# A state-space mixer with a LoRA feed-forward: TensorE's waits one product earlier, and work of the second batch moved between engines

## The reference

```python
proj = hidden_states @ in_proj_w.T
gate, hBC, dt = jnp.split(proj, [INTER, INTER + CONV_DIM], axis=-1)
hBC = silu(causal_conv4(hBC) + conv_b); hs, Bx, Cx = split(hBC)
dt = softplus(dt + dt_bias); A_dt = A * dt; A_cs = cumsum(A_dt) in each chunk
M = (Cc Bc^T) * exp(segsum(A_dt))          # mask of decays in a chunk
Y_diag = M X                               # X = hs * dt
states = (Bc * exp(A_cs[-1] - A_cs))^T X   # one state a chunk, passed on
Y_off = (Cc prev_states) * exp(A_cs)
xg = (Y_diag + Y_off + D * hs) * silu(gate)
xr = xg * rsqrt(mean over the 1024 channels of a group + EPS)
return (xr * norm_weight) @ out_proj_w.T
```

## Time and profile before

| | |
|---|---|
| median of 3 runs | 1581.26 us (1580.66 to 1581.79) |
| profiled execution | 1580.66 us, its span 1578.9 us |
| first batch, a step between group ends | 10.78 us |
| second batch, a step between group ends | 10.78 us |

### The profile page before, as it was taken

How to read it: one execution, slowest core, us unless ns; L and a number is a source line. 1 busy time by engine, 2 the same in 40 slices (tenths; PEclk the granted TensorE clock), 3 DMA queues, 4 the chain that set the end, 5 groups by cost and what they waited for, 6 DMA issues and landing times.

```text
span 1578.9 us, 29209 instructions
## 1 busy us (share of the span) xinstructions
PE 1559.5 (99%) x9172; PEld 1271.9 (81%) x9172; DVE 1414.5 (90%) x2343; ACT 1367.7 (87%) x2620; POOL 1291.1 (82%) x1614
## 2 busy tenths in 40 slices
PE   8999999999999999999999999999999999999998
PEld 7877888888888888887778788888888888888886
DVE  6988999999999999999979898898898888888887
ACT  4678899999999999989846899999999999999996
POOL 5549998999999998989874488778787878787786
PEclk9999999999999999999999999999999999999999
DMA  5257767676776676766614666766667667667673
GB/s 178 94 171 223 197 214 221 196 226 195 220 225 198 213 224 199 220 202 208 198 42 142 201 198 222 218 201 225 212 200 230 200 210 222 199 221 215 202 225 92
DMA packets 231754, 311.83 MB, mean 197 GB/s; under 512 B 144176, under 2 KB 160560, under 8 KB 231344
## 3 DMA queue, kind: packets, MB, share of 16 engines
q1 hardware_dynamic: 231600, 309.97, 63.9%
HBM read 240.69 MB, written 36.70 MB: 176 GB/s over the span
## 4 chain that ended last, share of the span: by engine, by line
PE 87%; DVE 5%; POOL 4%; issue 2%; ACT 1%; DMA 1%; SPq 0%; DVEq 0%; ACTq 0%; POOLq 0%
PE bg L804 21%; PE bo L975 20%; PE bt L804 12%; PE bh L804 11%; PE by L1031 7%; PE bg L1053 7%; PE bt L1018 3%; PE bh L1018 2%; PE bo L783 1%; POOL wl L631 1%; DVE cv L1085 1%; PE bo L862 1%; POOL xl L734 1%; DMA turned<-tg 1%; POOL wol L750 1%
## 5 line engine op out<-in xcount | busy, mean ns | idle before, releaser
L407 ACT ACTIVATE mt<-cs_row,cs_tok 128x128 f32<-128x128 f32 x1024 | 324.5, 390 | 0.0
L631 POOL TENSOR_TENSOR wl<-raw,wh 128x256 fp32r<-128x256 f32 x328 | 250.2, 792 | 59.1 <-ACT wh L379 59.1
L725 POOL COPY xt<-turned 128x512 uint16<-128x512 uint16 x248 | 202.3, 862 | 42.3 <-DMA turned<-tg 42.3
L716 POOL TENSOR_TENSOR mt<-mt,gt 128x256 f32<-128x256 f32 x128 | 118.0, 943 | 141.7 <-ACT mt L588 141.2
L741 POOL TENSOR_TENSOR sqa<-sqa,sq 128x256 f32<-128x256 f32 x222 | 223.7, 1027 | 1.0 <-ACT sq L561 1.0
L750 POOL TENSOR_TENSOR wol<-raw_o,woh 128x256 fp32r<-128x256 f32 x256 | 190.4, 764 | 10.5 <-ACT woh L528 10.5
L734 POOL TENSOR_TENSOR xl<-xg,xh 128x256 fp32r<-128x256 f32 x254 | 189.7, 768 | 6.0 <-ACT xh L541 6.0
L1085 DVE SCALAR_TENSOR_TENSOR cv<-bt,par_sb,cv 128x511 f32<-128x511 f32 (+2 forms) x192 | 143.7, 748 | 49.3 <-ACT cv L383 44.8
L1085 DVE SCALAR_TENSOR_TENSOR cv<-bh,par_sb,cv 128x511 f32<-128x511 f32 (+2 forms) x192 | 143.7, 748 | 35.4 <-ACT cv L383 30.9
L379 ACT ACTIVATE wh<-raw 128x1024 fp32r<-128x1024 f32 (+1 forms) x146 | 152.3, 1043 | 0.7 <-DMA raw<-in_w_dtag 0.7
L975 PE MATMUL bo<-woh,xl 128*128 128x512 f32 x508 | 149.1, 415 | 0.4 <-POOL xl L734 0.4
(11 more groups left out here) (215 smaller groups left out, 3814.7 us busy)
## 6 DMA issues: line engine op xcount, KB each, us to landing
raw<-in_w_step SPq DMA_DIRECT2D x128, 512.0 KB, 4.6
cs_row<-cs_rows SPq DMA_DIRECT2D x128, 512.0 KB, 7.0
low_parts<-wl SPq DMA_DIRECT2D x64, 512.0 KB, 5.8
raw_o<-in_w_out SPq DMA_DIRECT2D x128, 256.0 KB, 5.7
wl<-low_parts SPq DMA_DIRECT2D x64, 512.0 KB, 4.7
ec_row<-ec_rows SPq DMA_DIRECT2D x256, 96.0 KB, 5.7
raw<-in_w_bc SPq DMA_DIRECT2D x16, 512.0 KB, 3.6
acc<-in_x SPq DMA_DIRECT2D x8, 256.0 KB, 5.4
```

The lines of the kernel that those rows point to most:

```text
L407: e = act.activation(mt[:, m % 2, h, chunk(j)], cs_row[:, m % 2, h, chunk(j)], ACT.Relu, bias=cs_tok[:, j, 2 * m + h:2 * m + h + 1], scale ...
L631: e = pool.tensor_tensor(wl[:, n % 2, cols], raw[:, n % 2, cols], wh[:, n % 2, cols].bitcast(F32), ALU.subtract)
L725: e = pool.tensor_copy(to[:, half], turned[:, NJ * half:NJ * (half + 1), :])
```

## The change

1. TensorE, in the iterations with `early_state`: each wait stands one product earlier. The states' wait (v_xd) stands before the last wol product, p_xl's before the last of the states, the chunk products' (v_x, v_m or p_m, v_xg) before the last product with xl, those of the products with S (and of the sum of squares) before the last chunk product, and the next step's weights before the last product with S.
2. Second batch: GpSimd masks both heads, the first ahead of the tokens' copy, the second behind xl; VectorE masks none (but for the last step).
3. Second batch: VectorE drains two blocks of a group, ScalarE and GpSimd two.
4. First batch: `keep_high` stores wh in DRAM (512 KB a step) at the end of SP's iteration, and ScalarE's next split into the same buffer awaits it. Second batch: `load_parts` loads high and low part of the step's weights; raw isn't loaded and ScalarE makes no wh there.
5. `add_bias` moves from iterations 2 to 5 to the last four B and C units of the prologue.
6. VectorE's statistics and norm of the next batch move from behind the gate and convolution products to a place ahead of the taps.

```diff
+            def keep_high(m):
+                sp.wait_ge(a_wh, did(step(0, m)))
+                sp.dma_start(high_parts[m], wh[:, step(0, m) % 2, :].bitcast(F32)).then_inc(st_high[m % 2], 16)
+
+            def load_parts(m):
...
+                sp.wait_ge(st_high[m % 2], landed(m))
+                sp.dma_start(wh[:, step(1, m) % 2, :].bitcast(F32), high_parts[m]).then_inc(ld_high[m % 2], 16)
                 sp.wait_ge(st_low[m % 2], landed(m))
                 sp.dma_start(wl[:, step(1, m) % 2, :].bitcast(F32), low_parts[m]).then_inc(ld_low[m % 2], 16)
...
+        def dve_blocks(g):
+
+            return DVE_BLOCKS if g < GROUPS else 2
...
+                    if g >= GROUPS - NJ:
+                        add_bias(b, g - (GROUPS - NJ))
...
+                        if m < STEPS:
+                            mask_decays(0)
+                        else:
+                            mask_decays(1).then_inc(p_m, 1)
...
+                    if masks and m < STEPS:
+                        mask_decays(1).then_inc(p_m, 1)
...
                                 for j in range(NJ):
+                                    if then and k == ks[-1] and j == NJ - 1:
+                                        then()
...
                         if has(m - 2):
-                            output(range(2) if early_state else range(3))
+                            if early_state:
+                                output(range(2), await_states)
+                            else:
+                                output()
...
                         for c in range(NS):
+                            if early_state and c == NS - 1:
+                                pe.wait_ge(p_xl, did(n - 2))
                             mm = pe.matmul(other[:, chunk(c)], btok[:, g, c, :], xd[:, c, :], start=True, stop=True)
                         mm.then_inc(t_st, 1)
+                        yb = bank_y(b, m - 1)
                         if early_state:
-                            output((2,))
...
+                            output((2,), await_chunks, awaited=True)
+                        else:
+                            await_chunks()
                         for j in range(NJ):
                             for h in range(2):
+                                if early_state and j == NJ - 1 and h == 1:
+                                    if ends:
+                                        await_squares()
+                                    await_off()
...
+                            if c == 1:
+                                pe.wait_ge(v_s, did(n - 1, 4, 4))
+                            if c == NS - 1 and early_state and has(m + 1):
+                                await_weights(b, step(b, m + 1))
```

More of the change, by code:

```diff
@@ L189, in did, with by_dve, by_act @@
             return n * per + (CR + (per if k is None else k))
+        def dve_blocks(g):
+            return DVE_BLOCKS if g < GROUPS else 2
+        def by_dve(g, k=None):
+            return CR + sum(dve_blocks(i) for i in range(g)) + (dve_blocks(g) if k is None else k)
+        def by_act(g, k=None):
+            return CR + sum(NJ - dve_blocks(i) for i in range(g)) + (NJ - dve_blocks(g) if k is None else k) \
+                if g >= 0 else CR
         def landed(n):
@@ L367, in _ @@
                                 .then_inc(ld_ec[m % 2], 16)
+                    if b == 0 and has(m + 1):
+                        keep_high(m + 1)
             store(NB - 1)
@@ L377, in split_hi @@
             def split_hi(n):
+                b, m = step_of(n - 2)
+                if b == 0 and m >= 0:
+                    act.wait_ge(st_high[m % 2], landed(m))
                 act.wait_ge(ld_raw[n % 2], landed(n))
@@ L477, in _ @@
                     first_tap(b, g, 1, bank_c[g % 2])
-                    split_hi(bc(b, g + 2))
+                    if b == 0 or g + 2 < GROUPS:
+                        split_hi(bc(b, g + 2))
                     if g == 0:
@@ L590, in _ @@
                             take_b(b, GROUPS - 1)
-                    if has(m) and not early_split and (has(m + 2) or b + 1 < NB):
+                    if has(m) and not early_split and b + 1 < NB:
                         act.wait_ge(t_g, did(n))
@@ L736, in _ @@
                         e.then_inc(p_xl, 1)
+                    if masks and m < STEPS:
+                        mask_decays(1).then_inc(p_m, 1)
+                    if has(m - 2) and (b + 1 < NB or has(m - 1)):
                         if (m - 2) % PER_GROUP:
@@ L791, in tokens, with await_weights, project @@
                 return lambda k: t[:, b, k, :] if j is None else t[:, b, k, chunk(j)]
-            def project(dst, b, n, kind):
-                pe.wait_ge(a_wh, did(n))
+            def await_weights(b, n):
+                _, m = step_of(n)
+                if b == 1 and m >= 0:
+                    pe.wait_ge(ld_high[m % 2], landed(m))
+                else:
+                    pe.wait_ge(a_wh, did(n))
+            def project(dst, b, n, kind, awaited=False):
+                _, m = step_of(n)
+                kept = b == 1 and m >= 0
+                if not awaited:
+                    await_weights(b, n)
                 for i, (w, t) in enumerate(((wh, xTh), (wh, xTl), (wl, xTh))):
                     if i == 2:
-                        _, m = step_of(n)
-                        if b == 1 and m >= 0:
+                        if kept:
                             pe.wait_ge(ld_low[m % 2], landed(m))
@@ L934, in sum_squares, with await_states, await_chunks, await_squares @@
                         return mm
-                    def output(ks=range(3)):
+                    def await_states():
+                        pe.wait_ge(v_xd, did(n - 1))
+                        if not by_dma(b, m - 1):
+                            pe.wait_ge(v_x, did(n - 1))
+                        if m > 2 and (m - 2) % PER_GROUP == 0:
+                            pe.wait_ge(v_ms, did((n - 2) // PER_GROUP - 1))
+                        if m == 1:
+                            pe.wait_ge(a_bt, did(b * GROUPS + (GROUPS - 1)))
+                    def await_chunks():
+                        pe.wait_ge(v_x, did(n - 1))
+                        if b + 1 < NB:
+                            pe.wait_ge(v_m, did(n - 1))
+                        else:
+                            pe.wait_ge(p_m, m)
+                            if m == STEPS:
+                                pe.wait_ge(v_m, did(STEPS))
+                        if bank_y(b, m - 1) is by:
+                            pe.wait_ge(v_xg, did(n - 2))
+                    def await_squares():
+                        pe.wait_ge(v_h2, did(un))
+                        pe.wait_ge(p_sqa, squares(b, m - 2))
+                    def await_off():
+                        pe.wait_ge(v_sg, did(min(n, b * STEPS + STEPS - 1)))
+                        pe.wait_ge(v_off, did(n - 2))
+                        pe.wait_ge(a_s1, did(n - 1))
+                        pe.wait_ge(v_s, did(n - 1, 4, 2))
+                    def output(ks=range(3), then=None, awaited=False):
                         first, very_last = (m - 2) % PER_GROUP == 0, n - 2 == NB * STEPS - 1
@@ L982, in _ @@
                             pe.wait_ge(v_h2, did(un - 4 + m))
-                        project(mine, b, step(b, m), 0).then_inc(t_hs, 1)
+                        project(mine, b, step(b, m), 0, awaited=m > 2).then_inc(t_hs, 1)
                         if m == 0:
@@ L1111, in add_group @@
                 else:
-                    dve.wait_ge(p_acc, did(g - 1, ACT_BLOCKS))
-                for j in range(1, NJ) if very_last else range(DVE_BLOCKS):
+                    dve.wait_ge(p_acc, by_act(g - 1))
+                for j in range(1, NJ) if very_last else range(dve_blocks(g)):
                     if very_last:
@@ L1329, in _ @@
                         add_group(b, ended)
-                    if has(m - 1) and not ahead:
-                        mask_decays(2 if b + 1 < NB else 1)
+                    if has(m - 1) and b + 1 < NB:
+                        mask_decays()
                     if m == STEPS and b + 1 < NB:
@@ L1334, in _ @@
                         token_lo(b + 1, 3)
+                    if b + 1 < NB and STEPS - 12 <= m < STEPS - 6:
+                        h, part_of = divmod(m - (STEPS - 12), 3)
+                        if part_of < 2:
+                            stats_of(b + 1, 2 * h + part_of)
+                        else:
+                            variance(b + 1, h)
+                    if b + 1 < NB and STEPS - NJ <= m < STEPS:
+                        norm(b + 1, m - (STEPS - NJ))
                     if has(m):
```

112 lines of the change are left out of this document (45 added, 67 removed).

## The result

| kernel | median | ratio to before | profiled execution |
|---|---|---|---|
| before | 1581.21 us (5 runs) | | 1580.66, span 1578.9 |
| changed | 1606.33 us (1604.44 to 1609.15, 5 runs) | 1.0162 (95%: 1.0147 to 1.0176) | 1604.44, span 1602.5 |

The account below looks back on a forecast made before the run. TensorE's stream plus its stalls was taken as the bound; +1.7 + 4.2 - 2.7 - 2.4 - 1.1 = -0.3 us on the profiled 1580.66 gave 1580.4, by medians 1581.0 us, range 1564 to 1589.

Parts of the forecast that it names:

- The gaps are not waits: TensorE's idle 0.37 and 0.17 us around 64-column loads come from tiling changes; sooner waits gain 0 there.
- Part 1: TensorE's waits one product sooner, ordinary steps: 0 in the first batch, +1.7 us in the second for late xd.
- Rival C: Earlier xd wait at the last wol product costs a load's delay every step: +9.8 us, 1591; chance .18.
- Part 2: Group ends of the first batch: earlier waits for xd and S prolong the stalls, +4.2 us.
- Part 3: add_bias in the prologue relieves over-full GpSimd in steps 2 to 5, shortening waits for xd: -2.7 us.
- Part 4: VectorE's next-batch statistics ahead of the taps no longer delay S: -2.4 us.
- Part 5: Second batch, less work on ScalarE and VectorE: VectorE's relief returns S waits at group ends, -1.1 us.
- Part 6: High part stored in the first batch and reloaded in the second: both fit the DMA time, 0 us.
- Rival D: First batch: storing the kept high part delays the transposes, 62 x 0.1 to 0.3 us, 1587 to 1600; chance .08.

Follow-up runs that it names:

- safe_hoists: Changed kernel with the waits for xd and S (v_xd, v_s) at their old places, all others still early; 1581.8 us, ratio 1.0003.
- off_back: Changed kernel with the waits for S, sg, off, a_s1 and the squares at their old places, xd's still early; 1591.7 us, ratio 1.0066.
- hoist_only: Kernel before with TensorE's earlier waits alone and nothing else of the change; 1605.0 us, ratio 1.0147.
- all_back: Changed kernel with all of TensorE's waits at their old places, the rest as changed; 1581.0 us, ratio 1.0004.
- no_high: stats_back without the kept high part and its reload: raw is loaded and split in the second batch again; 1579.1 us, ratio 0.9986.
- bias_only: Kernel before with only add_bias moved to the prologue; 1579.3 us, ratio 0.9992.
- stats_back: all_back with VectorE's statistics and norm behind the convolution's product again; 1578.8 us, ratio 0.9984.
- yield_xd: Changed kernel, but GpSimd starts its second mask and its squares only when xd is done; 1598.7 us, ratio 1.0110.

## Why the prediction was wrong

It forecast no change and measured +25 us. Step by step, by its own parts:

- *The gaps are not waits*: right. 46.5 and 22.4 us after, 44.4 and 21.6 in safe_hoists. The rule of the Trainium skill (TensorEngine Tiling (Array Packing), Key Properties) that a change of tiling mode drains TensorE fits all of these runs. The early waits gained nothing at the four places that safe_hoists tests (the last of the states, the last product with xl, the last chunk product without v_s, the last product with S).
- *Part 1, ordinary steps, is the step that failed.* It took 0 in the first batch for xd, "a slip once a group, not once a step", because VectorE "has 0.54 to spare before its taps". This row reads [0.54 <-ACT cv L383], and that cv is made from TensorE's own projection of the same step. Idle time that ends with the bottleneck's own product is no slack against the bottleneck: if TensorE slips, the taps slip, and xd is as late in the next step as in this one. So the delay comes back step by step and not once a group. Measured with all waits early: 0.21 a step in the first batch, 0.31 in the second. Rival C had the place and the mechanism of xd, at 0.11 a step (13.6 us) and a chance of .18; off_back, where xd is awaited early and S isn't, has just that 0.11 in most steps of the first batch and puts the wait for xd at 10.7 us. What C lacked is the wait for S.
- *The wait for S was costed only at the ends of groups*; for an ordinary step part 1 put it at nothing without a reason. It is the larger one: 26 us alone. Most of what it needed was there: the first user of S's pieces stands two recorded products behind 1214.41, and the last chunk product, the new place, ahead of it; S's own row (1213.61) isn't among the rows of the prediction. The sentence "each wait stands one product earlier" was taken over for v_s without counting that it had stood at the second product behind the change of tile, 0.53 away. Nor did the prediction name the way over ScalarE, which is what makes S late in hoist_only's second batch.
- *Part 2, group ends*, +4.2: they aren't to be told apart from the loss in every step; eight steps grew by 1.6 and 1.9 us, of which the ordinary steps make the most.
- *Part 3, bias*, -2.7: the mechanism was right, the size 1.5.
- *Part 4, statistics*, -2.4: +2.2 measured. The statistics' half was right (-1.8). The norms wait for GpSimd's rstd, and I had not asked what would be queued behind that wait.
- *Part 5*, -1.1 at the second batch's group ends from VectorE's relief: the step behind each of them went from 10.98 to 10.78 (all_back), 1.4 us in seven. But VectorE's relief alone, in no_high, changed that step and the next from 10.99 and 10.78 to 10.81 and 10.88 and the batch by 0.4 (678.51 in bias_only to 678.13); the rest came with ScalarE's relief. That the size came near is partly luck, as the relief that counted was to the larger part ScalarE's. VectorE's mask, costed at 1.0, took 0.68 to 1.26 before. That the second mask would stand beside xd and not only beside the squares wasn't seen; with the waits at their old places it costs nothing (10.78), with them early it makes 10.95 into 11.09.
- *Part 6, the store*: right within what can be told (stats_back 1578.8, no_high 1579.1), though its two halves are +1.5 and -1.3 and not 0 and 0. Rival D falls: the transposes land as before (1.38 for 1.40).

## What to carry to other kernels

A wait in front of a product costs nothing as long as what it waits for comes in time, and gives nothing by standing earlier unless something behind it is held up; so count, for each semaphore, the time between its signal and its new place in the load queue, across every product and change of tile that it is moved over. Where the awaited chain begins with the bottleneck's own output of the same step, it is a loop: add it up once round, compare it with the bottleneck's own step, and take the whole excess for every step. Do it for each engine on which such a way leads back; when one loop is shortened, the next longest is the limit. And an operation that is moved ahead of others takes its waits with it: the question is what stands behind it in that queue.

## What the runs showed of the hardware

- The gap before the first load with another tile width is the same wherever the waits stand: 0.37 us from 128 to 64 columns behind a 512-column product, 0.17 back behind chunk products of 128. A late semaphore ahead of it can hide in it in part: in yield_xd the wait for the masks held the last load of xl by 0.21, the gap behind it shrank to 0.24, and the step grew by 0.04 (10.82).
- VectorE and GpSimd beside each other: xd takes 0.55 alone, 1.13 if a GpSimd piece of 0.74 starts 0.03 ahead of it, 1.01 if it starts 0.14 ahead and 0.81 if 0.35 ahead, so the less of the piece is left, the less xd pays. xt takes 1.04 with a piece that started 0.56 ahead and was 1.05 long, 1.26 with one of 0.74 that started 0.03 ahead; the norm took 0.53 before and 1.00 where it stands now. If the piece starts 0.11 or more behind xd, xd stays at 0.57 to 0.60 and the piece takes 1.06 for 0.74. So a few hundredths of a microsecond between the starts settle which of the two pays, and in this kernel's repeated step mostly the same way in each (1.06 to 1.14 in 47 of 59 steps of the changed kernel's second batch).
